# Routed expert results kept in slot order: plain stores, 32 gathers by slot, and four late shared chunks

## The reference

```python
logits = h @ router_w.T                       # 16 experts
top_vals, top_idx = jax.lax.top_k(softmax(logits), 4)
top_vals = top_vals / top_vals.sum(-1)
y = silu(h @ w_gate[e]) * (h @ w_up[e]) @ w_down[e]         # 176 hidden columns per expert
routed = sum over the 4 chosen experts of top_vals * y
shared = silu(h @ sh_gate) * (h @ sh_up) @ sh_down           # 704 hidden columns
out = x1 + routed + sigmoid(h @ sh_gate_w) * shared
```

## Time and profile before

| | |
|---|---|
| median of 3 runs | 393.48 us |
| lowest, highest | 391.77, 394.31 us |
| profiled execution, first to last instruction | 424.4 us |
| mean granted TensorE clock in it | 0.968 of full speed |
| PE, DVE, ACT, POOL busy in it | 382.7, 221.2, 147.6, 188.6 us |

### The profile page before, as it was taken

How to read it: one execution, slowest core, us unless ns; L and a number is a source line. 1 busy time by engine, 2 the same in 40 slices (tenths; PEclk the granted TensorE clock), 3 DMA queues, 4 the chain that set the end, 5 groups by cost and what they waited for, 6 DMA issues and landing times.

```text
span 424.4 us, 6202 instructions
## 1 busy us (share of the span) xinstructions
PE 382.7 (90%) x1984; PEld 328.6 (77%) x1984; DVE 221.2 (52%) x533; ACT 147.6 (35%) x304; POOL 188.6 (44%) x176
## 2 busy tenths in 40 slices
PE   3998869999999999999999996788987779999996
PEld 3877869787888888888777885687876668899885
DVE  6894554289512211221779763734454324656557
ACT  2644265244534433342554252412122111322140
POOL 0625653563255454423212277355665566444600
PEclk9999989999999999999989999898988898999999
DMA  6965353275233333111013785222222233111285
GB/s 213 386 253 165 101 175 113 74 260 192 88 114 124 125 124 124 39 38 37 2 37 101 181 195 169 62 73 70 85 88 74 72 90 85 61 57 64 77 317 190
DMA packets 22004, 51.89 MB, mean 122 GB/s; under 512 B 3878, under 2 KB 9510, under 8 KB 21670
## 3 DMA queue, kind: packets, MB, share of 16 engines
q1 hardware_dynamic: 16022, 35.24, 25.0%
q0 software_dynamic: 5952, 16.26, 12.6%
HBM read 38.12 MB, written 13.37 MB: 121 GB/s over the span
## 4 chain that ended last, share of the span: by engine, by line
PE 63%; DVE 11%; another core or an unknown queue 9%; DMA 5%; issue 5%; POOL 3%; ACT 2%; SPq 1%; POOLq 0%; DVEq 0%; ACTq 0%
PE gu L1500 9%; PE gu L1501 9%; PE gu L1502 9%; PE y L1889 7%; PE gu L1864 4%; PE gu L1868 3%; PE gu L1865 3%; PE y L1500 2%; PE y L1501 2%; PE y L1502 2%; PE gu L1526 2%; DMA w_raw<-y_k 1%; PE gu L1813 1%; PE gu L1791 1%
## 5 line engine op out<-in xcount | busy, mean ns | idle before, releaser
L591 POOL TENSOR_TENSOR w_lo<-w_raw,w_hi 128x768 fp32r<-128x768 f32 (+3 forms) x26 | 34.4, 1344 | 76.8 <-ACT w_hi L716 60.4
L681 POOL DMA_INDIRECT y_k<-w_raw,put x47 | 46.2, 984 | 49.9 <-DVE w_raw L1417 41.5
L1500 PE MATMUL gu<-act_hi,w_hi 128*128 128x512 f32 x132 | 53.6, 406 | 0.8 <-DVE hid L1023 0.8
L1501 PE MATMUL gu<-act_lo,w_hi 128*128 128x512 f32 x132 | 52.4, 397 | 0.0
L1864 PE MATMUL gu<-w_hi,xgT 128*128 x94 | 40.3, 429 | 12.1 <-ACT xgT L899 8.7
L1023 DVE TENSOR_TENSOR hid<-silu,gu 128x512 f32<-128x512 f32 x24 | 16.5, 687 | 66.6 <-PE gu L1502 66.5
L1502 PE MATMUL gu<-act_hi,w_lo 128*128 128x512 f32 x124 | 48.9, 394 | 0.0
L944 ACT ACTIVATE silu<-gu 128x176 f32<-128x176 f32 x47 | 14.9, 317 | 90.7 <-PE gu L1868 55.8
L1410 DVE TENSOR_TENSOR hid<-silu,gu 128x176 f32<-128x176 f32 x47 | 15.7, 334 | 48.8 <-ACT silu L944 30.6
L1865 PE MATMUL gu<-w_lo,xgT 128*128 x94 | 32.2, 343 | 0.0
L745 ACT ACTIVATE hid_hi<-hid 128x512 fp32r<-128x512 f32 x24 | 15.2, 631 | 47.3 <-DVE hid L1023 47.3
(11 more groups left out here) (325 smaller groups left out, 905.3 us busy)
## 6 DMA issues: line engine op xcount, KB each, us to landing
w_raw<-in_w_gu SPq DMA_DIRECT2D x16, 352.0 KB, 4.6
w_raw<-in_wc SPq DMA_DIRECT2D x8, 576.0 KB, 5.0
w_raw<-y_k SPq DMA_DIRECT2D x5, 512.0 KB, 5.7
w_hi_f<-in_w0s SPq DMA_DIRECT2D x6, 368.0 KB
y_k<-hid SPq DMA_DIRECT2D x1, 2048.0 KB, 13.3
w_dn<-in_w_dn SPq DMA_DIRECT2D x1, 1936.0 KB
w_raw<-in_ws SPq DMA_DIRECT2D x5, 384.0 KB, 3.0
w_hi_f<-y_k SPq DMA_DIRECT2D x6, 256.0 KB, 4.4
```

What stands on the lines that cost most here:

```text
L591: nc.gpsimd.tensor_tensor(w_lo[par][:, w], w_raw[par][:, w], w_hi[par][:, w].bitcast(F32), ALU.subtract).then_inc(split, 1)
L681: nc.gpsimd.indirect_dma_start(d["y_k"], bass.IndirectOffsetOnAxis(ap=put[:, i:i + 1], axis=0), t_out[j], None).then_inc(s_y[j], 16)
L1500: T.matmul(out, w[0], x[0], start=start, stop=False)
L1501: T.matmul(out, w[0], x[1], start=False, stop=False)
```

## The change

`NA` goes from 4 to 2: chunks 2 and 3 of the shared network join chunk 4 and the tail behind the tiles ("four late chunks"). A tile's result is stored by SP with a plain DMA, in slot order (`y_k[i * 128:(i + 1) * 128]`), and POOL does one gather a tile and no scatter. At the end POOL waits for all stores and issues 32 gathers, one for each of 8 token tiles and 4 choices, that fetch rows of `y_k` by the slot of the choice (`slot_i`). The gather ring is 8 buffers with 5 tiles of lead (`GET_AHEAD`). The diagonal sums on PE and ACT are gone: DVE adds all 32 choices. The tables `put`, `choice`, `empty` shrink to layer 0's use. The raw weights of chunk 4 and the tail are loaded when the last tile's gate/up product is done (`late_raw`). The late down products of all four chunks use the unsplit float32 form.

```diff
-NA = 4
+NA = 2
...
-            for j in range(RING):
-                sp.wait_ge(s_y[j], Y_BEFORE[j] + 16 * len(range(j, SLOT_TILES, RING)))
+            for i in range(SLOT_TILES):
+                if i == SLOT_TILES - DOWN_BACK:
+                    sp.wait_ge(t_gu, SLOT_TILES)
+                    for k in range(2):
+                        sp.dma_start(late_raw[k], d["w"][SH][NA + 2 + k]).then_inc(s_raw[(C0[SH] + NA + k) % 2], 16)
+                sp.wait_ge(t_put, i + 1)
+                sp.dma_start(d["y_k"][i * P:(i + 1) * P], t_out[i % RING]).then_inc(s_y[i % RING], 16)
             for t in range(NT):
-                sp.dma_start(y_in[t], d["y_k"][0:N * K1].rearrange("(n k) h -> n k h", k=K1)[t * P:(t + 1) * P]
-                             ).then_inc(s_fin[t], 16)
-            for t in range(NT):
-                sp.wait_ge(s_fadd[t], K1 + 1 if t < ON_PE else 2)
+                sp.wait_ge(s_fadd[t], K1 + 1)
                 sp.dma_start(d["out"][t * P:(t + 1) * P], base(t)).then_inc(s_out, 16)
...
             def gather(i, j):
-                if i >= XG:
-                    pool.wait_ge(t_xT, i - XG + 1)
+                if i >= GET_AHEAD:
+                    pool.wait_ge(t_xT, i - GET_AHEAD + 1)
...
+            def choice_rows(t, k):
+                landed = s_rows[0] if last_choice(t, k) else t_in[t]
+                nc.gpsimd.indirect_dma_start(y_in[t][:, k], None, d["y_k"],
+                                             bass.IndirectOffsetOnAxis(ap=slot_i[:, k, t:t + 1], axis=0)).then_inc(landed, 16)
...
+            for i in range(SLOT_TILES):
                 gather(i, i % XG)
-            for i in range(SLOT_TILES):
-                step(i, i % RING)
+            for j in range(RING):
+                pool.wait_ge(s_y[j], 16 * len(range(j, SLOT_TILES, RING)))
+            for t in range(NT):
+                for k in range(K1):
+                    choice_rows(t, k)
...
-            shared_gu(2, 0)
             shared_dn(1, 1)
             spread_gate(1)
-            shared_gu(2, 1)
-            shared_dn(2, 0)
-            shared_gu(3, 0)
-            shared_dn(2, 1)
+            pe.wait_ge(s_sgb, 2)
             turn_in(0)
-            shared_gu(3, 1)
             turn_in(1)
...
             pe.wait_ge(t_hd, SLOT_TILES)
+            late_gate_up(NA, 0)
+            late_gate_up(NA, 1)
+            pe.wait_ge(t_put, SLOT_TILES)
+            for k in LATE_K[1:]:
+                for s in range(2):
+                    late_down(k - 1, s)
+                    late_gate_up(k, s)
             for s in range(2):
+                late_down(NC[SH] - 1, s)
...
+            add_choices(0)
+            late_product(NA + 1, 0)
+            add_choices(1)
+            late_product(NA + 1, 1)
+            add_choices(2)
+            late_product(NA + 2, 0)
+            add_choices(3)
+            late_product(NA + 2, 1)
+            late_product(NA + 3, 0)
+            add_choices(4)
+            late_product(NA + 3, 1)
+            for t in range(5):
+                add_shared(t, K1)
+            for t in range(5, NT):
+                add_shared(t, 0)
+            for t in range(5, NT):
+                add_choices(t, 1)
```

More of the change, by code:

```diff
@@ L51 @@
 RING = 4
-XG = 16
+XG = 8
 LEAD = 2
@@ L55 @@
 DOWN_BACK = 4
[L56 removed]
+GET_AHEAD = 5
 DEPTH = 4
@@ L1351, in _ @@
             shared_low(1, 1)
-            chain(V.scalar_tensor_tensor(out=empty[:], in0=got[:], scalar=0.0, in1=cst1[:, CT_DUMP:CT_DUMP + SLOT_TILES],
-                                         op0=ALU.is_equal, op1=ALU.mult))
-            chain(V.tensor_scalar(choice[:], get_i[:], N.bit_length() - 1, None, ALU.arith_shift_right))
-            chain(V.scalar_tensor_tensor(out=y_row[:], in0=get[:], scalar=float(K1), in1=choice[:], op0=ALU.mult, op1=ALU.add))
-            V.tensor_tensor(put[:], y_row[:], empty[:], ALU.add)
-            gate_up_low(3)
             dim = [1, SLOT_TILES, E1]
@@ L1929, in _, with late_gate_up @@
                 tile_down(i, of[i])
-            def late_gate_up(s):
-                k4 = c + NA
-                pe.wait_ge(s_wg, k4 + 1)
-                if s:
-                    pe.wait_ge(s_prod, 2 * (c + NA) + 2)
+            def late_gate_up(k, s):
+                n = 2 * (c + k) + s
+                if s == 0:
+                    pe.wait_ge(s_wg, c + k + 1)
+                if k > NA:
+                    pe.wait_ge(s_prod, n - 1)
+                w = late_w(k)[1:]
+                if is_tail(k):
+                    for h in range(KH):
+                        ins = mm3(GU[s][0][:], parts(w, A, slice(h * P, (h + 1) * P)), parts(ACTV, A, h, half(s)), h == 0, h == KH - 1)
+                    ins.then_inc(s_u, 1)
+                    return
@@ L1941, in late_gate_up, with late_down @@
                     ins.then_inc(done, 1)
-            def late_tail(s):
-                k5 = c + NA + 1
-                pe.wait_ge(s_wg, k5 + 1)
-                for k in range(KH):
-                    ins = mm3(late_ps[2 + s][0][:], parts((w_hi[k5 % 2], w_lo[k5 % 2]), A, slice(k * P, (k + 1) * P)),
-                              parts(ACTV, A, k, half(s)), k == 0, k == KH - 1)
-                ins.then_inc(s_u, 1)
-            def late_down(q, s, tail):
-                par, u = (c + q) % 2, 2 * (q - NA) + s
-                pe.wait_ge(s_prod, 2 * (c + NA) + LATE.index(u) + 1)
+            def late_down(k, s):
+                pe.wait_ge(s_prod, 2 * (c + k) + s + 1)
+                of = rows(is_tail(k))
@@ L1954, in late_down @@
                 for t in range(NT // 2):
                     ins = T.matmul(Y[t // 2][s][:, (t % 2) * H:(t % 2 + 1) * H],
-                                   late_hid[u][rows(tail), t * P:(t + 1) * P], w_raw[par][rows(tail), dn_cols(SH)],
-                                   start=tail and t % 2 == 0, stop=not tail and t % 2 == 1)
+                                   late_hid[late_buf(k, s)][of, t * P:(t + 1) * P], late_w(k)[0][of, dn_cols(SH)],
+                                   start=k == NA and t % 2 == 0, stop=is_tail(k) and t % 2 == 1)
```

229 lines of the change are left out of this document (94 added, 135 removed).

## The result

The changed kernel takes **415.11 us** (median of 4 runs, 412.79 to 416.48), the kernel before 392.62 us beside it (4 runs, 391.56 to 394.31). The ratio is 1.0564, 95% interval 1.0513 to 1.0616: 22.5 us slower. The forecast was 410.4 us in a range of 402.5 to 418.

The account below looks back on a forecast made before the run. PE was taken to bound the kernel up to the end, a chain of reload, adds and store. Front -7.3, tile stage -0.5 and end +24.7 gave +16.9 on 393.5: 410.4 us, range 402.5 to 418.

Parts of the forecast that it names:

- the 30 us of waits: Tile stage: six long waits of ACT's silu in the first profile, 30.0 us in total, assumed absent from timed runs.
- Rival (c): Tile stage: ACT's waits come from scatter and gather alternating on POOL and vanish, all six giving 380 us; chance 0.04.
- Front, -7.3 (-4.5 to -10): Ahead of tile 0 and its first steps: less shared work, start limited by the first gathers, 7.3 us saved.
- Tile stage, -0.5 (0 to -2): Tile stage: without scatters POOL no longer falls behind PE, and nobody waits for the plain stores; 0.5 us saved.
- The end, +24.7: From PE's first late gate/up matmul to the end: 49.8 us against 25.05 before, bounds +18.2 to +36.
- POOL's side: The end: 32 gathers in a row after the last store, 48.3 us, plus 1.5 for contention with DVE's adds.
- PE's side: The end if gathers cost nothing: late matmuls, DVE's adds behind them and the last store, 43.3 us.
- (a): The end: gathers issue 1.1 us apart or less, so PE's late work sets the end, 403.9 us; chance 0.15.
- (b): The end: each gather is delayed by one DVE add, 12.8 us instead of 1.5, giving 421.7 us; chance 0.08.
- (d): Front: nothing gained, as first tiles starve on gathers with a lead of 5, giving 417.7 us; chance 0.05.
- What would show it: Signs forecast for the changed kernel's profile, among them tile 0's gate/up 5 to 7 us earlier and gathers 1.27 us apart.

Follow-up runs that it names:

- before_again: The kernel before, unchanged, timed and profiled once more: 394.12 us, ratio 1.0024, span 393.2 us.
- after_again: The changed kernel, unchanged, timed and profiled once more: 438.65 us against 421.36 for the kernel before, ratio 1.0407.
- low_after: The changed kernel with DVE's two 1408-column subtractions held back until the first three gathers have landed: 419.35 us, ratio 1.0637.
- dn_after: The changed kernel with the load of the down weights held back until the first two gathers of tile rows have landed: 420.85 us, ratio 1.0696.
- scatter_slots: The changed kernel with tile results stored by GpSimd's indexed stores instead of SyncE's plain ones, 8 gathers ahead, then alternating: 467.94 us, ratio 1.1845.
- end_8_more: The changed kernel with 8 more indexed loads of 128 rows ahead of the 32 at the end: 425.17 us, ratio 1.0808.
- end_plain: The changed kernel with the 32 indexed loads at the end replaced by 8 plain loads of 512 KB: 409.14 us, ratio 1.0373.
- late_third: The changed kernel with one matmul instead of three for each late gate/up product in the three whole late chunks: 415.46 us, ratio 1.0550.
- ahead_8: The changed kernel with gathers of tile rows allowed 8 tiles ahead instead of 5: 413.73 us, ratio 1.0495.

## Why the prediction was right, and where it missed

**What bounds the kernel, and the 30 us of waits.** Right for the 393 us in question: `before_again` shows none. The rounds of `after_again` suggest that timed runs can have such waits too: the kernel before took 28.7 us more there. Rival (c) falls all the same: the changed kernel, which has no scatters in its tile stage, has such waits in its profile of these rounds, and stays slower.

**Front, -7.3 (-4.5 to -10): measured -2.8 to -4.4, outside its bounds.** The term has two parts: 5.9 us by which tile 0 starts earlier, and 1.4 for the two down halves in steps 0 and 1. Tile 0 came 3.7 us earlier behind the routing matmuls, 2.1 to 2.4 against the two profiles of before at full clock. From tile 0 to tile 5 it is 13.72 us instead of 14.40, at a granted clock of 0.50 up to 255 us, so the down halves gave 0.7. The mechanism was right (gathers, not PE's work, set tile 0's start), the size was not. The step that failed is "Served in order, the first gather is in at about 246, the second at about 248.5". It read the bytes of POOL's queue as if the rows arrived in the order of their gathers, and gave the first 5.4 us of flight; even with the allowance that the prediction makes, the second gather was to be in 9.4 to 10.9 us after the first one's issue, and it took 13.3. The runs show 10.8 us for the first beside the load of down weights (11.2 in `low_after`) and 3.5 without it (`dn_after`). The load was in flight there, at a DMA share of 0.79; what a gather pays for that can't be read from bytes, and `dn_after` was the way to ask. How the DMA engines share their time between the two is not shown. I also left out that the first issues would take 1.6 to 2.4 us, having seen 1.96 in the earlier trace rows; `low_after` shows that this does not set the landings.

**Tile stage, -0.5 (0 to -2): measured -0.3.** The stage is 1.0 us shorter, of which 0.7 are the down halves above. From tile 5 to tile 46 it is 92.60 us instead of 92.95 in `before_again`. Tiles stay 2.26 us apart in both, but for one step of 2.57 us in the kernel before. What the plain stores are worth depends on the ring, though: with 8 buffers and scatters in their place the time is 53 us longer (`scatter_slots`), with the 16 buffers and the lead of 22 of the kernel before the scatters cost 0.3. That the stores are what makes the small ring, and with it the late chunks' memory, possible follows from these two, not from a run of its own.

**The end, +24.7: measured +24.9.** POOL's side was 49.8 with 48.3 from its steps. Measured: start at T0 + 4.9 (taken 3.4), 31 intervals in 39.45 us (taken 39.4 + 1.5 for contention; 0.7 of it is contention beyond 31 x 1.25), 5.85 from the start of the last gather to the end (taken 5.5). That none of the tile stores is waited for was not quite so: the copy of the last tile's result waited 1.1 us for a buffer that a store still held. The slope of 1.26 us for each gather (`end_8_more`) shows that the issues are in series on GpSimd. The errors of +1.5 at the start and -1.5 in the block cancel, so the closeness of the total is partly luck. PE's side, 43.3, is 43.5 in `end_plain`, and its T0 + 33.7 is met there to the tenth. Behind it two errors cancel again: no product queues behind adds there (0.6 taken), but a choice add takes 0.50 us and not 0.40, so the work of DVE behind PE's end is 7.6 us instead of 6.5. In the changed kernel PE ends at T0 + 36.7, since DVE's order hands it the gathers' pace (`late_third`).

**Rivals.** (a), cheap issues and PE's side: excluded by `end_8_more`. The Trainium skill, "DMA: Bandwidth & Descriptors", section "Anatomy of one DMA — SWDGE (gpsimd) path", calls descriptor generation "small, variable". The trace does not agree for these gathers: each takes 0.94 us of GpSimd, 1.25 with its gap. (b), one add of delay for each gather: 5 of the 32 gathers took 1.04 to 1.18 us and the rest 0.94 or 0.95, 0.7 us in all against the 12.8 that (b) asks. (c), above. (d), the front gives nothing through a lead of 5: `ahead_8` shows the lead is not the cause, though a part of (d)'s effect, 2.9 us or more of the 7.3, came by another way.

**What would show it.** Met: PE idles ahead of tile 0 on gathers, the pitch of 2.26, the block of 32, PE done over 10 us early, adds of token tile 7 on DMA, POOL in the chain. Not met: tile 0 came 3.7 us earlier relative to the routing matmuls, not 5 to 7. The total was 4.7 us above the forecast. As a difference the miss is larger, +22.5 against +16.9, since the kernel before came out 0.9 us faster than the 393.5 that the sum starts from. Of the +21.2 between the two profiles, 4.3 were not forecast: 2.9 in the front's two parts, 1.05 in the stretch ahead of it, which the change does not touch, and 0.4 in the rest.

## What to carry to other kernels

Indexed transfers have a price per instruction on the engine that issues them, here 1.25 us for 128 rows of 1 KB. Spread over a long stage beside PE they were hidden, gathered at the end behind one "all stored" wait they are a chain of 40 us. Work moved off the front gains only down to the next wait; look at when the first transfers land and at which loads are in flight beside them, and measure how long a transfer takes beside them; the sum of bytes did not tell it here. And an instruction that waits, placed ahead of another chain's work in one engine's order (adds before products, a store before a gather), joins the two chains.

## What the runs showed of the hardware that was not expected

- Beside a load on 88 partitions the DMA share was 0.66 and the rate 144 GB/s; with the same load issued as 80 + 8 partitions 0.97 and 207 GB/s. The profile doesn't say which engines each used.
- A gather of 128 rows of 1 KB lands 3.5 us after its issue without that load, and beside it 9.8 to 11.8 (the first two in `before_again`, the changed kernel and `low_after`) or 14.6 to 18.8 (the third to seventh in `dn_after`).
- A gather's issue takes 2.30 and 2.36 us beside DVE subtractions of two SBUF operands (1.60 us), and 0.95 without them.
- In one set of rounds both kernels took longer in all timed runs, by 28.7 and 23.5 us in the medians, and the one profile from it has two waits of ACT, 16.0 and 20.5 us, without a visible releaser. Their cause stays open.
- In `before_again` the granted clock was 0.50 for some 3 us in which PE was busy throughout; in the first profile of the same kernel it was 1.00 there.
